# A decoder kernel: ScalarE's order in the rounds of the pairs, a shorter opening of TensorE, and no unread matmul behind the last pair

## What is computed

```python
x = x + _L0_attn_ref(_layernorm(x), ...)      # 16 heads of 128, causal, with ALiBi
x = x + _L0_xattn_ref(_layernorm(x), ctx_2048, mask, ...)   # 16 heads of 16 over 1500 keys
x = x + _L0_ffn_ref(_layernorm(x), ...)       # ternary gate/up/down, 8-bit rounding, Hadamard transform
x = x + _L1_attn_ref(_layernorm(x), ...)      # 16 heads of 16, 4 of keys and values
x = x + _L1_xattn_ref(_layernorm(x), ctx_2048, ...)   # a decayed sum over the context, in closed form
x = x + _L1_ffn_ref(_layernorm(x), ...)       # 256 -> 1024 -> 256, h rounded to tenths, gelu
```

## Time and profile before

| | before |
|---|---|
| median of 3 runs | 502.4 us (500.69 to 503.15) |
| the profiled execution, its own time | 503.83 us |
| its span | 502.0 us |
| PE busy | 475.0 us (95%) |
| DVE busy | 363.7 us (72%) |
| ACT busy | 322.2 us (64%) |
| chain that ended last | PE 73%, DVE 15%, ACT 6%, issue 4%, DMA 1% |
| pieces of PE on that chain near its end | `hidden(2)` 3.83 us, the hidden parts 7.16, `keep_warm(4)` ahead of `turn_x7(3)` 0.86, the two matrices of the last step 2.04 + 0.89 + 0.89 + 3.47 |
| mean granted clock of PE | 0.993 |

### The profile page before, as it was taken

One profiled execution on the slowest core, in us unless ns is written; L12 is line 12 of the kernel. 1 busy time (PEld: TensorE's weight loads), 2 busy tenths in 40 slices (PEclk: granted clock), 3 DMA queues, 4 the chain that ended last, 5 costly groups with the idle time before them and its releaser, 6 DMA issues.

```text
span 502.0 us, 16406 instructions
## 1 busy us (share of the span) xinstructions
PE 475.0 (95%) x7067; PEld 406.5 (81%) x7067; DVE 363.7 (72%) x817; ACT 322.2 (64%) x594; POOL 4.2 (1%) x15
## 2 busy tenths in 40 slices
PE   8999999999898999999999999899999899986897
PEld 7999999998787888888878878778878787674575
DVE  5666887788566755567956678965878965797973
ACT  4777787778563666567666567666666656445744
POOL 1000000000000000000000000000000000000000
PEclk9999999999998999999999999999999999998999
DMA  6466441202301221111111111111111100000000
GB/s 198 143 233 249 153 154 48 63 23 98 134 5 41 50 72 51 43 43 43 43 44 43 44 43 43 44 42 44 43 44 44 43 3 3 3 1 0 1 10 28
DMA packets 12236, 30.86 MB, mean 61 GB/s; under 512 B 1666, under 2 KB 4867, under 8 KB 11396
## 3 DMA queue, kind: packets, MB, share of 16 engines
q1 hardware_dynamic: 11716, 29.08, 18.4%
q0 software_dynamic: 192, 0.51, 0.3%
q10 hardware_dynamic: 256, 0.23, 0.1%
HBM read 29.35 MB, written 0.46 MB: 59 GB/s over the span
## 4 chain that ended last, share of the span: by engine, by line
PE 73%; DVE 15%; ACT 6%; issue 4%; DMA 1%; DVEq 0%; SPq 0%; ACTq 0%
PE psb L1438 12%; PE psb L1428 11%; PE psa L1499 9%; PE psa L1347 7%; PE psb L1517 7%; PE psa L1360 4%; PE pst L1369 3%; PE psb L1400 3%; PE psa L1380 2%; ACT shared L625 2%; PE psa L1759 1%; PE pst L1584 1%; DVE st L777 1%; PE psb L1391 1%; DVE shared L993 1%
## 5 line engine op out<-in xcount | busy, mean ns | idle before, releaser
L1438 PE MATMUL psb<-wkv,cx 128*125 128x256 f32 x576 | 80.4, 288 | 5.5 <-ACT kx L463 5.5
L1438 PEld LDWEIGHTS psb<-wkv,cx 128*125 128x125 f32 x576 | 71.0, 186 | 8.1 <-ACT kx L463 6.6
L1428 PE MATMUL psb<-cx,wkv 128*128 128x500 f32 x276 | 74.6, 405 | 0.2 <-ACT vmem L470 0.2
L470 ACT ACTIVATE vmem<-psb 125x512 f32<-125x512 f32 x45 | 26.8, 596 | 55.1 <-PE psb L1438 55.1
L1428 PEld LDWEIGHTS psb<-cx,wkv 128*128 128x128 f32 x276 | 48.3, 188 | 12.0 <-ACT vmem L470 0.3
L1499 PE MATMUL psa<-qb,kx 32*125 32x112 f32 x1536 | 55.7, 282 | 0.8 <-ACT shared L625 0.6
L1499 PEld LDWEIGHTS psa<-qb,kx 32*125 32x125 f32 x1536 | 47.2, 186 | 8.3 <-issue 3.7
L993 DVE TENSOR_SCALAR shared<-shared,top 125x896 f32<-125x896 f32 x48 | 30.8, 684 | 31.6 <-ACT shared L625 31.3
L625 ACT ACTIVATE smem<-psa 125x1792 f32<-125x1792 f32 x23 | 38.3, 1667 | 14.3 <-PE psa L1499 14.3
L993 DVE TENSOR_SCALAR smem<-smem,top 125x896 f32<-125x896 f32 x48 | 30.8, 683 | 21.8 <-ACT smem L625 21.2
L625 ACT ACTIVATE shared<-psa 125x1792 f32<-125x1792 f32 x24 | 40.0, 1666 | 10.4 <-PE psa L1499 10.1
(11 more groups left out here) (341 smaller groups left out, 830.3 us busy)
## 6 DMA issues: line engine op xcount, KB each, us to landing
ring<-ctx_t_dram SPq DMA_DIRECT2D x24, 500.0 KB, 3.5
whd<-wqk_dram SPq DMA_DIRECT2D x16, 256.0 KB, 2.7
qb<-wvp_dram SPq DMA_DIRECT2D x8, 256.0 KB, 2.9
whd<-wo_dram SPq DMA_DIRECT2D x16, 128.0 KB, 2.7
wraw<-w_dram SPq DMA_DIRECT2D x2, 1024.0 KB, 5.9
mats_sb<-mats_dram SPq DMA_DIRECT2D x1, 1536.0 KB, 10.0
wraw<-gate_dram SPq DMA_DIRECT2D x1, 1024.0 KB, 6.7
wraw<-up_dram SPq DMA_DIRECT2D x1, 1024.0 KB, 7.2
```

What stands on the lines that cost most here:

```text
L470: nc.scalar.activation(vu[u % 2][:, 2 * r:2 * r + 2, :, 0:XD], bank[0:CT, :].rearrange("p (t h d) -> p t h d", t=2, d=XD), ACT.Copy).then_ ...
L1428: last = nc.tensor.matmul(bank[:, 0:UT], wkv[a][:, 0, c, m * P:(m + 1) * P], cx[b][u % 2][:, c, :], start=(a == b and c == 0), stop=(a == ...
L1438: last = nc.tensor.matmul(bank[0:CT, t * D:(t + 1) * D], cx[b][u % 2][:, c, a0:a0 + CT], wkv[a][:, 1, c, :], start=(a == b and c == 0), st ...
```

## The change

- ACT in a round: `move_xnT(1..3)` (rounds 2, 4, 6) ahead of `round_up`. A new function `first(t, o)` behind `move_k`: `root(2, t)` at o = 2 (before: at the end of the round before), `move_y2(t)` at o = 8 (before: at the end of the round before), `root(5, t)` at o = 14 (before: at the end of o = 13). `root(3, t)` goes from the front to the end of round o = 2.
- In rounds 17, 29 and 41 (`BEHIND`) `move_k` is DVE's (`take_k`), behind `remainder`.
- DVE in a round: `add_delta(t)` (o = 2) and `quantise_hidden(t)` (o = 8) stand between `clip` and `weigh`; before, `add_delta` was ahead of `clip`, and `quantise_hidden` behind `weigh`.
- Behind the last pair: all 53 matmuls of `keep_warm` are gone. `hidden_part(2)` comes behind `hidden_part(1)` on PE. `root(5, 3)` goes ahead of the table load of `gelu(2)` on ACT. `last_add(1)` and its output come ahead of `last_add(2)`.
- The opening of PE: 6 of the 18 fp32 matmuls stay, then come 8 of 128x128 in fp32r, and 16 of 32 rows and 112 columns in fp32r, four groups of rows in turn, into four places of PSUM.

```diff
+            def first(t, o):
+                if o == 2:
+                    root(2, t)
+                if o == 8:
+                    move_y2(t)
+                if o == 14:
+                    root(5, t)
...
-                if s >= 2 and u + 1 < B * UPB:
+                if s >= 2 and s not in BEHIND and u + 1 < B * UPB:
                     move_k(u + 1, r, kvb)
+                if s in (2, 4, 6):
+                    move_xnT(s // 2)
+                for t in reversed(range(NT)):
+                    first(t, s - 12 * (t + 1))
                 if r == 0 and s not in SILU and u + 2 < B * UPB:
                     round_up(u + 2)
                 if s in (1, 3, 5):
                     root(1, s // 2 + 1)
-                if s in (2, 4, 6):
-                    move_xnT(s // 2)
...
+            def take_k(u, m):
+                dve.wait_ge(s_kp, 2 * u + m + 1)
+                dve.wait_ge(s_qk, 2 * u - 2)
+                nc.vector.tensor_scalar_add(kx[u % 2][:, m, :], kvb[:, 0:UT], cols_sb[:, 1, m:m + 1]).then_inc(s_ke, 1)
...
+                if s in BEHIND:
+                    take_k(s // 2 + 1, 1)
...
                 clip(s)
+                for t in reversed(range(NT)):
+                    between(t, s - 12 * (t + 1))
                 weigh(s // 2, s % 2)
...
-            for _ in range(18):
+            rounded = ones.bitcast(F32R)
+            for _ in range(6):
                 nc.tensor.matmul(T0[:, 0:P], ones[:, :], ones[:, :], start=True, stop=True)
+            for _ in range(8):
+                nc.tensor.matmul(T0[:, 0:P], rounded[:, :], rounded[:, :], start=True, stop=True)
+            for k in range(16):
+                g = 32 * (k % 4)
+                nc.tensor.matmul(PS[k % 4][:, 0, 0:TT], rounded[g:g + 32, :], rounded[g:g + 32, 0:TT], start=True, stop=True, tile_position=(g, 0))
...
-            keep_warm(12)
             pe.wait_ge(s_kve, 7)
             hidden_part(0, 0)
...
-            keep_warm(1)
-            hidden_part(2, 0)
-            hidden_part(2, 1)
             pe.wait_ge(s_z, 6)
             hidden_part(1, 0)
             hidden_part(1, 1)
-            keep_warm(4)
+            hidden_part(2, 0)
+            hidden_part(2, 1)
             turn_x7(3)
-            keep_warm(1)
```

More of the change, by code:

```diff
@@ L31 @@
 SILU = (16, 28, 40)
+BEHIND = (17, 29, 41)
 FF = 1024
@@ L295, in _ @@
                 sp.dma_start(ctxs[u % 3], ctx_t[u]).then_inc(s_ctx[u % 3], 16)
-            for i, t in enumerate((0, 2, 1, 3)):
-                sp.wait_ge(s_fin, i + 1)
+            for t in range(NT):
+                sp.wait_ge(s_fin, t + 1)
                 sp.dma_start(out[t * TT:(t + 1) * TT, :], xs[:, t, :]).then_inc(s_out, 16)
@@ L583, in early @@
                     move_ctxT(t)
-                if o == 2:
-                    root(3, t)
                 if o == 3:
@@ L598, in late @@
             def late(t, o):
-                if o == 1:
-                    root(2, t)
+                if o == 2:
+                    root(3, t)
                 if o == 4:
                     back()
-                if o == 7:
-                    move_y2(t)
                 if o == 8:
@@ L615, in late @@
                     move_aT(t)
-                if o == 13:
-                    root(5, t)
                 if o == 16:
@@ L705, in _ @@
             move_aT(3)
+            root(5, 3)
             nc.scalar.preload_act_table(ACT.Gelu_apprx_tanh)
@@ L708, in _ @@
             back()
-            root(5, 3)
             root(6, 3)
@@ L1165, in last_add @@
             def last_add(t):
-                dve.wait_ge(s_fo, (1, 3, 2, 4)[t])
+                dve.wait_ge(s_fo, t + 1)
                 nc.vector.tensor_tensor(xs[:, t, :], xs[:, t, :], bank_fo[t][0:TT, 0:D], ALU.add).then_inc(s_fin, 1)
@@ L1173, in early @@
                     centre_delta(t)
-                    add_delta(t)
                 if o == 4:
@@ L1191, in early, with between @@
                     normalise7(t)
+            def between(t, o):
+                if o == 2:
+                    add_delta(t)
+                if o == 8:
+                    quantise_hidden(t)
             def late(t, o):
@@ L1200, in late @@
                     scale_hidden(t)
-                if o == 8:
-                    quantise_hidden(t)
                 if o == 9:
@@ L1308, in _ @@
             add_normalised(3)
+            last_add(1)
+            normalise7(3)
             last_add(2)
-            normalise7(3)
-            last_add(1)
             for k in range(4):
@@ L1703, in late @@
                     turn_attended(t)
-            def keep_warm(n):
-                for _ in range(n):
-                    nc.tensor.matmul(kvb, identb[:, :], wter[:, 0, 0:512], start=True, stop=True)
             for s in range(PAIRS - 2):
@@ L1770, in _ @@
             weighted_values(PAIRS - 1)
-            keep_warm(3)
             turn_context(3)
             nc.tensor.matmul(A3[0:TT, 0:D], minus[:, :], bias2[:, 0:D], start=True, stop=False)
-            keep_warm(4)
             turn_divided(3)
             project_in(2)
-            keep_warm(1)
             pe.wait_ge(s_cTe, 8)
@@ L1795, in _ @@
             hidden(1, 0)
-            keep_warm(2)
-            keep_warm(3)
             for half in range(2):
```

## The result

| | before | changed |
|---|---|---|
| median, range of 15 runs each | 501.55 us (500.69 to 503.74) | 503.4 us (500.96 to 507.96) |
| ratio of the times | | 1.0044 [1.0025, 1.0064] |
| the profiled execution, its own time | 503.83 us | 502.33 us |
| its span, mean granted clock | 502.0 us, 0.993 | 500.5 us, 0.973 |
| PE busy | 475.0 us | 469.5 us |

The change costs about 1.9 us where 5.6 were forecast to be gained: 503.4 lies above the range. By the 0.5% bound it is "same", but the interval is clear of 1. What follows reads where the time lies from the profiles, and how much it is worth from the times.

What follows compares the result with a forecast made beforehand. PE was taken to bound the kernel for three quarters of the chain, so its waits counted. Terms -3.4 - 2.0 - 0.5 + 0 - 1.6 + 1.9 = -5.6 took the 502.4 us median to 496.8, range 494.2 to 501.0.

Steps and rivals of the forecast that it cites:

- Round 2, -3.4: `move_xnT` ahead of `round_up` on ACT: `project_q` no longer waits for the load, `project_k` starts 3.4 us earlier.
- Rounds 20, 32, 44, -2.0: `move_y2` behind `move_k`: exponential starts earlier, PE's wait for `kx` goes, `turn_xq2` starts earlier; -0.65 us each.
- Rounds 14, 26, 38, -0.5: Roots behind `move_k` and `add_delta` behind `clip`: +0.1 us in round 14, -0.3 each in rounds 26 and 38.
- it waits 0.2: Round 26: with `add_delta` behind `clip`, PE waits 0.2 us for `xq`, leaving 0.3 us of gain.
- the lateness ends: DVE, 1.16 us late after round 26, makes it up in its idle time in round 28, before the gate's scaling.
- Rounds 17, 29, 41, 0: `move_k` moved to DVE: 0.1 us new gain in round 29 against +0.1 for a later ring load; sum 0.
- most landings are near the median: Ring loads behind `weigh(29)`: 4.5 us landings would cost PE 0.7 us in round 31, 3.5 nothing; +0.1 taken.
- Behind the last pair, -1.6: After the last pair: unread matmuls removed from the chain give 1.55 us, the new order little more, as DVE is late next.
- The clock, +1.9: Lowered PE clock after new quiet stretches: +1.0 us after the opening, +0.9 behind the last pair.
- 0.1 for shorter ones: Behind the last pair, clock loss from PE's shorter quiet stretches: 0.1 us, beside 0.4 each for two longer ones.
- more of the low clock: Rival: three quiet stretches each cost their full 1.7 us, +5.1 instead of +1.9, giving 500.0 us; chance 0.12.
- "slower" rival: Rival: the low clock level stays on behind the last pair, slowing PE's pieces near the chain's end, 511.5 us; chance 0.06.

Runs made afterwards that it cites:

- unread_off_chain: The kernel before with the changed kernel's order edits and without 10 of its 53 unread matmuls, chiefly those on the chain: 498.1 us, ratio 0.992.
- unread_off_chain_more: As unread_off_chain, with 15 unread matmuls added in PE's waits, 10 ahead of `turn_xq2` and 5 ahead of the gate's scaling: 497.17 us, ratio 0.99.
- roots_undone: The changed kernel with the old opening and all 53 unread matmuls, but the rounds' roots and `add_delta` in their old places: 497.48 us, ratio 0.9905.

## Why the prediction was wrong, point by point

- **Round 2, -3.4: mechanism right, size off.** The profile pair shows 4.0 in rounds 2 and 3. But the median gained 1.6. The step that failed is taking the lowered clock of the earlier trace rows, and the whole 2.21 us of PE's wait, into the term as if every execution had them. The sum was made against one execution that was 2.3 us above the median of 15, and rounds 2 and 3 alone held 2.5 us more than in the two profiles without the fall.
- **Rounds 20, 32, 44, -2.0: right.** 0.73 to 0.75 each in the profile, 2.3 by the times.
- **Rounds 14, 26, 38, -0.5: wrong sign, +0.8.** Round 26 went as worked out. The failed steps are "it waits 0.2" and "the lateness ends" in round 28. The exponential started 0.1 us later in its round and DVE 0.2 later than worked out, the wait was 0.29, and with the lost overlap of two transposes the price was 0.49; then round 29 cost 0.4 more.
- **Rounds 17, 29, 41, 0: nearly right against before, +0.4.** Rounds 29 to 31 are 19.25 us for 19.15, and 41 to 43 are 19.43 for 19.09. The price named for a late ring load came in round 43, where `round_up` waited 1.87 us for the load and the round grew from 6.88 to 7.65, and 0.3 of it in round 31. The failed step is "most landings are near the median": in round 43 every profile with `take_k` had the wait.
- **Behind the last pair, -1.6: about twice too large.** The unread matmuls on the chain were not 1.55 us but some 0.8 in the trace of `unread_off_chain`, and 0.2 by its times. For the rest, PE most likely arrives sooner at a wait for DVE or ACT. The new order there shows nothing by itself: from pair 47 to the end the two profiled kernels of the old order with all 53 have 77.8 us, those of the new 77.4 to 78.2. `turn_x7(3)` did wait for DVE as forecast, 1.31 us, and `root(6, 3)` did take back what `root(5, 3)` gave: DVE's wait for the root is 1.33 us where it was 1.32. A drain behind a table load did not show either. The Trainium skill, "ScalarE: Activation LUTs", "What ACT_TABLE_LOAD costs", has 2.66 us for both; here the trace disagrees, since ACT's next row stands 1.30 behind the start of the load (484.58, then `root` at 485.88).
- **The clock, +1.9: the main miss.** The opening costs 2.6 (forecast 1.0), above even the 1.7 that was its upper bound: that was the loss of one short fall, and the low level lasted from 8 us to 14.7. "Six are 2.1 us at that mean" was off as well; they took 2.93, since the first of the 18 run slower than their mean. The unread matmuls cost 2.9 net, with the old opening; forecast were -1.55 for them and +0.9 of clock, -0.65. With 0.8 for what stood on the chain, the clock there cost some 3.7, an estimate from 2.9 and 0.8. The failed step is "0.1 for shorter ones": there were falls where PE had only waits of 0.5 to 0.9 us behind it too, as in the stretch of 0.86 from 424 us. The rival "more of the low clock" had the cause and 500.0 us; with round 2 at its real worth of 1.6 instead of 3.4 it would have said 501.8, still short of 503.4. The "slower" rival had the low level stay on. It did not stay: it fell and came back several times, and from 472 us on the clock was 0.99 and above. So none of the three signs of being wrong came up (round 29 at 5.2 us, a wait left in round 2, 0.50 beyond 480), and the time still lay outside the range: no sign stood for many short falls.
- **A slip in the rivals.** With `project_k` at 157 instead of 155.5 the forecast would be 1.5 higher, 498.3, not 498.8. It changes nothing.

The account by the times, from 501.5: order edits -3.1, opening +2.6, unread matmuls +2.9, 503.9; measured 503.4. Of the -3.1, single edits give -1.6, -2.3, -1.4 and +0.8, -4.5 in all. The difference of 1.4 is about the overlap of `take_k` and the roots that their stretches show. What each reordering behind the last pair (`hidden_part(2)`, `root(5, 3)`, `last_add`) does by itself wasn't tried. Nor was `unread_off_chain_more` with the roots undone, which these numbers would put near 496.3, an estimate from 497.17 and the 0.84 of `roots_undone`.

What the Trainium skill has in "TensorE: Matmul & The Clock Gate", Part 1, that the half rate is the default and activity releases it, agrees with all of this: the kernels without unread matmuls ran longer at granted clocks of 0.973 and 0.979, and the one with the most in its waits had 1.000. I had cited it, and given its extreme form 0.06 and the milder rival 0.12.

## What to carry to other kernels

Matmuls that nobody reads can be worth more than the time they take on the chain. Before removing them from the path, ask how the useful ones behind them run without them, and price the fall of the clock at every wait that they covered, not at the longest three. And compare the profiled execution with the median of many runs before its rare features go into a sum: a low stretch in one trace is a chance, not a term. Where two kernels differ by about 1 us, look first at the stretches in which their code is the same; here one such round differed by up to 1.3. An edit that moves work on the fuller engine behind a step should be followed for three rounds, as what it gains in one it paid in the next.
